# A bf16 split of K and Q moved from GpSimd to TensorE and ScalarE, and small weight operations moved from VectorE to GpSimd

## The reference

```python
def attn(Q, K, V):                     # per item and head
    scores = einsum('bhqd,bhkd->bhqk', q, k) / sqrt(16)
    return einsum('bhqk,bhkd->bhqd', softmax(scores), v)

def fp4_quant_dequant(x):              # blocks of 16 along the last dim
    scale = maximum(max(abs(xb)) / 6, 1e-12)
    q = _GRID[searchsorted(_MID, abs(xb / scale))] * sign(xb) * scale

def ffn(x, w_gate, w_up, w_down):      # 256 -> 704 -> 256
    h = silu(fp4_linear(x, w_gate)) * fp4_linear(x, w_up)
    return fp4_linear(h, w_down)

x = x + attn(layernorm(x), ctx, ctx)
x = x + ffn(layernorm(x), w_gate, w_up, w_down)
```

## Time and profile before

| | us |
|---|---|
| median of three runs | 637.24 (634.64 to 638.73) |
| the profiled execution | 639.48 |
| its span, first to last instruction | 637.7 |
| attention, filling and draining included | to about 320 |
| feed-forward | about 320 to the end |

### The profile page before, as it was taken

How to read it: one execution, slowest core, us unless ns; L and a number is a source line. 1 busy time by engine, 2 the same in 40 slices (tenths; PEclk the granted TensorE clock), 3 DMA queues, 4 the chain that set the end, 5 groups by cost and what they waited for, 6 DMA issues and landing times.

```text
span 637.7 us, 13644 instructions
## 1 busy us (share of the span) xinstructions
PE 559.7 (88%) x3780; PEld 343.7 (54%) x3780; DVE 536.4 (84%) x1186; ACT 353.4 (55%) x656; POOL 434.6 (68%) x530
## 2 busy tenths in 40 slices
PE   1479999999999999999888999999999999999996
PEld 1235545555554554555546665665665665666664
DVE  1598999999999999986578889889889889889863
ACT  1226778777777777777635355354354354354341
POOL 7787788878788888723256766766766766766740
PEclk9999999999999999999998999999999999999997
DMA  7834443444434444310000000000000000000000
GB/s 233 187 101 134 134 131 113 125 118 133 123 109 121 118 117 125 100 52 3 1 0 10 9 18 16 8 16 16 8 16 16 8 16 14 10 16 8 17 17 25
DMA packets 43797, 40.61 MB, mean 64 GB/s; under 512 B 4728, under 2 KB 43512, under 8 KB 43768
## 3 DMA queue, kind: packets, MB, share of 16 engines
q1 hardware_dynamic: 43768, 40.26, 22.3%
HBM read 10.55 MB, written 4.19 MB: 23 GB/s over the span
## 4 chain that ended last, share of the span: by engine, by line
DVE 45%; PE 25%; issue 18%; ACT 4%; DVEq 3%; POOL 2%; DMA 1%; SPq 1%; ACTq 0%; POOLq 0%
DVE MF L573 8%; DVE QS L763 7%; PE PV L906 6%; PE MX L888 5%; PE SC L874 5%; DVE hmax L773 4%; DVE hinv L641 3%; DVE KS L791 3%; PE T L810 2%; DVE hinv L645 2%; ACT QS L521 2%; PE SC L988 2%; PE T L860 2%; DVE stats L581 2%; DVE QS L719 1%
## 5 line engine op out<-in xcount | busy, mean ns | idle before, releaser
L573 DVE TENSOR_REDUCE MF<-MX 128x2 f32<-128x512 f32 x256 | 168.6, 678 | 19.6 <-PE MX L888 19.0
L482 ACT ACTIVATE P<-SC 128x512 f32<-128x512 f32 x256 | 146.6, 607 | 22.1 <-PE SC L874 20.0
L888 PE MATMUL MX<-KS,QS 96*128 96x256 bf16 x512 | 104.9, 290 | 19.3 <-DVE MF L573 15.6
L988 PE MATMUL SC<-KS,QS 128*128 128x256 f32 x384 | 93.8, 395 | 17.2 <-ACT QS L537 17.2
L874 PE MATMUL SC<-QS,KS 98*128 98x256 bf16 x512 | 100.7, 279 | 0.5 <-ACT P L482 0.5
L988 PEld LDWEIGHTS SC<-KS,QS 128*128 128x128 f32 x384 | 72.0, 194 | 42.7 <-ACT QS L537 33.8
L432 POOL TENSOR_TENSOR QS<-QS 128x256 f32<-128x256 f32 (+1 forms) x47 | 48.4, 1029 | 56.9 <-ACT QS L532 35.8
L906 PE MATMUL PV<-P,VA 128*32 128x256 f32 x1024 | 82.0, 393 | 0.7 <-ACT P L482 0.4
L888 PEld LDWEIGHTS MX<-KS,QS 96*128 96x128 bf16 x512 | 46.9, 101 | 43.7 <-DVE MF L573 34.3
L874 PEld LDWEIGHTS SC<-QS,KS 98*128 98x128 bf16 x512 | 38.3, 99 | 57.0 <-ACT P L482 36.2
L432 POOL TENSOR_TENSOR KS<-KS 128x704 f32<-128x704 f32 x16 | 26.9, 1681 | 40.9 <-ACT KS L532 40.9
(11 more groups left out here) (109 smaller groups left out, 1112.8 us busy)
## 6 DMA issues: line engine op xcount, KB each, us to landing
KS<-KP SPq DMA_DIRECT2D x96, 128.0 KB, 2.4
QS<-QP SPq DMA_DIRECT2D x96, 128.0 KB, 2.4
X<-in_x SPq DMA_DIRECT2D x16, 256.0 KB, 2.9
C<-in_ctx SPq DMA_DIRECT2D x16, 256.0 KB, 3.1
out<-KS SPq DMA_DIRECT2D x16, 128.0 KB, 1.7
out<-QS SPq DMA_DIRECT2D x16, 128.0 KB, 1.7
W<-in_L_ffn_w_down SPq DMA_DIRECT2D x1, 704.0 KB, 8.0
W<-in_L_ffn_w_gate SPq DMA_DIRECT2D x1, 640.0 KB, 5.0
```

Source lines behind the costliest of these rows:

```text
L482: nc.scalar.activation(P[g % 2][:, j, :, :], SC[h % 3][:, :, :], ACT.Exp, scale=0.25).then_inc(exp_done, 1)
L573: nc.vector.tensor_reduce(MF[st.slot(off, 2)][:, :, h:h + 1], MX[h % 2][:, :, :], AX.X, ALU.max, negate=True).then_inc(mx_done, 1)
L888: last = nc.tensor.matmul(MX[h % 2][:, q, :], QS[r][0:PROD, h, q * 128:(q + 1) * 128], KS[r][0:PROD, h, :], start=True, stop=True)
L988: last = nc.tensor.matmul(DP, HT[r][:, c, :], WDT[:, c, :], start=(c == 0), stop=(c == NT - 1))
```

## The change

K is first copied by GpSimd into head-parity order in fp32 (KN), as QN is already. `flip` transposes KN or QN in fp32 into one PSUM bank (TA for K, TB for Q). ScalarE copies the bank to bf16, which is part 0. TensorE subtracts this part from the bank by a matmul with a negative identity (`rest`), ScalarE copies again for part 1, and once more for part 2. KB, QB and REST and both splits go. The variance, the limits and the floor of the weights go from VectorE to GpSimd. Several slots move, and the maxima's transposes go from TB to TA.

```diff
@@ gpsimd, attention_step
-                    pool.wait_ge(k_tr, st.times(LEAD - 2, 2, 2))
-                    pool.wait_ge(q_parts, st.times(LEAD, 1))
+                    pool.wait_ge(k_tr, st.times(LEAD, 3))
                     gate(pool)
-                    split(lambda q: by_parity(C[rc][:, q, :]), KB[r], 0, k_parts, st)
+                    for q in range(QT):
+                        nc.gpsimd.tensor_scalar(KN[:, q, :, :, :], by_parity(C[rc][:, q, :]), 1.0, 0.0,
+                                                ALU.mult, ALU.add).then_inc(kn_ready, 1)
+                    pool.wait_ge(stats_seq, st.times(LEAD, 4, 4))
+                    gate(pool)
+                    nc.gpsimd.tensor_scalar(ve[r][:, :], mv[:, :, 1], EPS, None, ALU.add).then_inc(ve_ready, 1)
                     pool.wait_ge(ve_ready, st.times(LEAD, 1, 1))
...
-                    split(lambda q: QN[:, q, :, :, :], QB[r], 5, q_parts, st)
...
+                    pool.wait_ge(w_abs, st.times(LEAD - 1, 1, 1))
                     gate(pool)
+                    nc.gpsimd.tensor_scalar(WC[:, :], WC[:, :], MAGIC * ONE, 0.0, ALU.max, ALU.add).then_inc(w_c, 1)
...
+                    pool.wait_ge(w_seq, st.times(LEAD, 4, 1))
+                    gate(pool)
+                    for dst, up in ((wscale[st.slot(LEAD, 2)], 1), (winv, UP)):
+                        nc.gpsimd.tensor_scalar(dst[:, :], wmax[:, :], up / 6, TINY * up,
+                                                ALU.mult, ALU.max).then_inc(w_seq, 1)
                     pool.wait_ge(w_seq, st.times(LEAD, 4, 4))
@@ scalar, attention_step
-                        if (g, j) == (0, 1) and st.has(LEAD - 1):
+                        if (g, j) == (0, 0) and st.has(LEAD - 1):
...
-                        if (g, j) == (1, 0) and st.has(LEAD):
-                            part_out(KP[st.slot(LEAD, 2)], 0, k_tr, k_out, st)
-                        if (g, j) == (1, 2) and st.has(LEAD):
-                            part_out(KP[st.slot(LEAD, 2)], 1, k_tr, k_out, st)
-                        if (g, j) == (1, 0) and st.has(LEAD):
-                            part_out(KP[st.slot(LEAD, 2)], 2, k_tr, k_out, st)
-                        if (g, j) == (0, 2) and st.has(-1):
+                        for n, at in enumerate(((0, 1), (1, 0), (1, 2))):
+                            if (g, j) == at and st.has(LEAD):
+                                part_out(KP[st.slot(LEAD, 2)], TA, n, k_tr, k_out, st)
+                        if (g, j) == (0, 3) and st.has(-1):
                             evacuate(st, -1, 1)
+                        for n, at in enumerate(((2, 0), (2, 2), (3, 1))):
+                            if (g, j) == at and st.has(LEAD):
+                                part_out(QP[st.slot(LEAD, 2)], TB, n, q_tr, q_out, st)
                         if (g, j) == (2, 3) and st.has(0):
                             evacuate(st, 0, 0)
-                        if (g, j) == (3, 1) and st.has(LEAD):
-                            part_out(QP[st.slot(LEAD, 2)], 0, q_tr, q_out, st)
-                        if (g, j) == (3, 3) and st.has(LEAD):
-                            part_out(QP[st.slot(LEAD, 2)], 1, q_tr, q_out, st)
-                        if (g, j) == (3, 3) and st.has(LEAD):
-                            part_out(QP[st.slot(LEAD, 2)], 2, q_tr, q_out, st)
@@ vector, attention_step
-                        if (g, j) == (0, 2) and st.has(LEAD):
-                            variance(st)
...
-                        if (g, j) == (1, 2) and st.has(LEAD):
-                            weight_limits(st)
...
-                        if (g, j) == (2, 0) and st.has(-1):
+                        if (g, j) == (2, 1) and st.has(-1):
                             denominators(st, 0)
-                        if (g, j) == (2, 1) and st.has(-1):
                             output(st, 0)
-                        if (g, j) == (2, 2) and st.has(1):
+                        if (g, j) == (2, 3) and st.has(1):
                             maxima_out(st)
-                        if (g, j) == (2, 2) and st.has(-1):
+                        if (g, j) == (3, 1) and st.has(-1):
                             denominators(st, 1)
-                        if (g, j) == (2, 2) and st.has(-1):
                             output(st, 1)
-                        if (g, j) == (1, 3) and st.has(LEAD - 1):
-                            round_weights(st)
@@ tensor
+            def flip(bank, src):
                 for e in range(2):
                     for q in range(QT):
+                        at = e * S + q * 128
+                        last = nc.tensor.matmul(bank[:, at:at + 128], src[:, q, e, :, :].rearrange("p d a -> p (d a)"),
+                                                ident[:, :], start=(at == 0), stop=False, is_transpose=True,
+                                                skip_group_check=True)
                 return last
+            def rest(bank, part, last):
+                return nc.tensor.matmul(bank, negidentb[:, :], part, start=False, stop=last, skip_group_check=True)
+            def keys(st, n):
+                if n == 0:
+                    pe.wait_ge(kn_ready, st.times(LEAD, QT, QT))
+                    pe.wait_ge(o_norm, st.times(-1, 2))
+                    flip(TA, KN).then_inc(k_tr, 1)
+                else:
+                    pe.wait_ge(k_out, st.times(LEAD, 3, n))
+                    rest(TA, KP[st.slot(LEAD, 2)][:, n - 1, :], n == 2).then_inc(k_tr, 1)
...
             def maxima(st):
                 pe.wait_ge(m_parts, st.times(1, 1, 1))
...
+                if st.has(-1):
+                    pe.wait_ge(o_norm, st.times(-1, 2, 1))
...
             def outputs(st, q):
...
                 pe.wait_ge(o_norm, st.times(-1, 2, q))
+                if q == 1 and st.has(1):
+                    pe.wait_ge(mt_ready, st.times(1, 1, 1))
...
-                        if (g, j) == (1, 1) and st.has(LEAD):
-                            keys(st, 0)
-                        if (g, j) == (1, 1) and st.has(LEAD):
-                            keys(st, 1)
+                        for n, at in enumerate(((0, 0), (0, 3), (1, 2))):
+                            if (g, j) == at and st.has(LEAD):
+                                keys(st, n)
+                        for n, at in enumerate(((1, 3), (2, 2), (3, 0))):
+                            if (g, j) == at and st.has(LEAD):
+                                queries(st, n)
...
-                        if (g, j) == (2, 3) and st.has(-1):
+                        if (g, j) == (3, 0) and st.has(-1):
                             outputs(st, 1)
-                        if (g, j) == (3, 0) and st.has(LEAD):
-                            queries(st, 0)
-                        if (g, j) == (3, 2) and st.has(LEAD):
-                            queries(st, 1)
```

More of the change, by code:

```diff
@@ L119, in program @@
         QN = sb("QN", [128, QT, 2, DK, H // 2])
-        REST = sb("REST", [128, QT, 2, DK, H // 2])
-        KB = [sb(f"KB{r}", [128, 3, QT, 2, DK, H // 2], bf16) for r in range(2)]
-        QB = [sb(f"QB{r}", [128, 3, QT, 2, DK, H // 2], bf16) for r in range(2)]
+        KN = sb("KN", [128, QT, 2, DK, H // 2])
         KP = [sb(f"KP{r}", [128, 3, 512], bf16) for r in range(2)]
@@ L178, in program @@
         TA, TB = T[:, 0, :], T[:, 1, :]
[L179 removed]
+        TA16 = TA.bitcast(bf16)
         GP = [MX[0][:, :, :].rearrange("p q s -> p (q s)")[:, 0:FH], SC[0][:, :, :].rearrange("p q s -> p (q s)")[:, 0:FH]]
@@ L358, in _ @@
             pool.wait_ge(consts, CONSTS)
-            def split(source, parts, seq, done, st):
-                for q in range(QT):
-                    nc.gpsimd.tensor_scalar(parts[:, 0, q, :, :, :], source(q), 1.0, 0.0,
-                                            ALU.mult, ALU.add).then_inc(parts_seq, 1)
-                pool.wait_ge(parts_seq, st.times(LEAD, 10, seq + 2))
-                for q in range(QT):
-                    nc.gpsimd.tensor_tensor(REST[:, q, :, :, :], source(q), parts[:, 0, q, :, :, :],
-                                            ALU.subtract).then_inc(parts_seq, 1)
-                rest = REST[:, :, :, :, :].rearrange("p q e d a -> p (q e d a)")
-                second, third = (parts[:, n, :, :, :, :].rearrange("p q e d a -> p (q e d a)") for n in (1, 2))
-                pool.wait_ge(parts_seq, st.times(LEAD, 10, seq + 4))
-                gate(pool)
-                nc.gpsimd.tensor_scalar(second, rest, 1.0, 0.0, ALU.mult, ALU.add).then_inc(parts_seq, 1)
-                pool.wait_ge(parts_seq, st.times(LEAD, 10, seq + 5))
-                nc.gpsimd.tensor_tensor(third, rest, second, ALU.subtract).then_inc(done, 1)
             def attention_step(st):
@@ L587, in aggregate @@
                     nc.vector.bn_aggr(mv[:, q, :], stats[:, q, :]).then_inc(stats_seq, 1)
-            def variance(st):
-                dve.wait_ge(stats_seq, st.times(LEAD, 4, 4))
```

(8 more changed lines are left out.)

72 lines of the change are left out of this document (20 added, 52 removed).

## The result

The changed kernel takes 640.95 us (median of 6 runs, 638.46 to 643.13) against 635.10 for the kernel before on the same chip (6 runs, 634.02 to 638.73): ratio 1.0083, 95% interval 1.0055 to 1.011. The forecast was 633.1, that is 4.1 less than the 637.24 from which it started; it is a small loss of 5.85 us.

A forecast was written before the change was run, and what follows sets the result against it. No engine was full; order inside the step bound the kernel, then the loop through K's copy. Steps 1 to 12 -2.3, step 0 -0.5, filling -1.7, steps 13 and 14 +0.4: -4.1, 637.24 to 633.1; range 623 to 641 us.

The forecast's parts named there:

- The new wait: TensorE, before the fp32 transposes of K: waits about 1.0 us in each step for GpSimd's K copy.
- the stall before max 5: TensorE idle 0.78 us before slot 5's pair of maxima matmuls, because the variance held up reduce 3; forecast to vanish.
- The low part: VectorE's low part of the maxima: forecast to fall from 1.10 to 0.19 us once GpSimd's last split goes.
- The new loop: Repeated step, through K's copy behind the addition to X: period 13.14 + 3.88 = 17.02 us, against 17.13.
- from the start of max 13 to the transposes: From slot 13's maxima matmuls through reduction, output 1, addition and K copy to TensorE's transposes of K: 3.88 us.
- The floor: Grid floor of the weights on GpSimd: 0.45 us taken, between 0.29 and 0.79, hidden in GpSimd's idle time.
- The filling: Before step 0: -1.7 us, of which 0.1 from earlier issue, ends -0.3 and -3.
- step 0: First attention step, no additions behind it; TensorE's slower matmuls hide VectorE's gain in its first half: -0.5 us.
- A: Rival: the loop without the two waits inside it, VectorE's starts being earlier; period 16.21, 623.3 us; chance 0.22.
- B: Rival: TensorE binds, the K copy being in time; period 16.05, 622.4 us; chance 0.08.
- C: Rival: GpSimd's late weight chain holds VectorE's cast or low part, +0.8 in each of 12 steps; 641 to 643; chance 0.13.
- D: Rival: transposes and subtractions at their high ends, +0.8 us per step on TensorE; about 641; chance 0.07.

The follow-up runs named there:

- Experiment 1: Changed kernel with GpSimd's copy of K for the next item issued before both additions to X, GpSimd's program loop covering steps 1 to 8: 628.79 us, ratio 0.9855.
- Experiment 3: Changed kernel with one more half copy of K, into a buffer nobody reads, right before GpSimd's copy of K: 654.17 us, ratio 1.027.
- Experiment 8: Changed kernel with denominators and output of half 1 one slot earlier on VectorE, from (3,1) to (3,0): 631.69 us, ratio 0.9914.
- Experiment 6: Kernel before with only variance, limits and floor moved to GpSimd, the split of K and Q left there too: 672.84 us, ratio 1.0585.
- experiment 2: Changed kernel with only the grid floor of the weights back on VectorE at its old slot: 637.88 us, ratio 1.0029.
- experiment 7: Changed kernel with variance, limits and floor all back on VectorE, so only the split remains changed: 642.23 us, ratio 1.0078.

## Why the prediction was wrong

**The mechanism held.** The new wait is where the prediction put it, of the size it gave (0.92 to 1.00 against "about 1.0"), released by K's copy right behind the addition. The maxima's transposes wait for the output; the variance's 0.8 and the stall before max 5 are gone. Experiments 1, 3 and 8 show the loop causally: open it and the period falls by 1.19; lengthen it by a copy of 0.6 and it grows by 0.56 to 0.60 where TensorE's clock holds; take the output out of it and it falls by 1.02.

**Many terms were right.** K's copy with fp32 output 1.22 (1.23 taken); a subtraction of 512 columns 0.22 in the queue; a group of fp32 transposes 0.44 where nothing holds it (0.43); variance 0.23 and limits 0.31 and 0.28 (0.2 each).

**The low part.** It fell from 1.10 to 0.19, as forecast. So its length was not its own. Experiment 6 keeps GpSimd's splits but shifts them against VectorE, and there it is short as well, while the cast before it is longer (durations in ns, min/median/max, of experiment 6, and one of its steps):

```profile
L618 DVE CAST MP<-MF x16: 173/418/1090, 46.2 to 326.8; 128x32 bf16<-128x32 f32 x16
L623 DVE TENSOR_TENSOR MP<-MF,MP x16: 191/192/364, 46.6 to 327.0; 128x32 bf16<-128x32 f32 x16
...
122.12 0.62 POOL L374 TENSOR_SCALAR QB<-REST 128x512 bf16<-128x512 f32 x1 [0.20 <-POOL REST L368]
122.35 0.42 DVE L618 CAST MP<-MF 128x32 bf16<-128x32 f32 x1
122.80 0.19 DVE L623 TENSOR_TENSOR MP<-MF,MP 128x32 bf16<-128x32 f32 x1
122.82 1.19 POOL L376 TENSOR_TENSOR QB<-REST,QB 128x512 bf16<-128x512 f32 x1
```

The overlap alone doesn't hold it; what differs is which starts first. In before the low part starts 0.10 behind GpSimd's last subtraction (126.13 and 126.03) and ends 0.05 after it; here it starts 0.02 ahead of the same subtraction and takes 0.19. The Trainium skill (SBUF — State Buffer, Who interferes with whom) says that a VectorE instruction with two SBUF inputs contends with a GpSimd instruction that reads SBUF; the low part, with its two inputs, agrees. The cast has one input, and by these rows it seems held as well: it starts behind GpSimd's copy and ends 0.03 after it (122.77 and 122.74).

**What failed is the length of the loop, in sum 17.02 where 17.57 was measured.** I said I would be wrong over 17.5. The 0.55 is no single error, but more than half of it is one kind of term, the hops from one instruction to the next, and one of them I had read from the wrong place:

```
term of "The new loop"                           forecast  measured
output 1 to the addition to X                        0.09     0.19
addition and the hop to K's copy                     0.69     0.80
from the start of max 13 to the transposes           3.88     4.07
transposes of K, first slot behind the wait          0.43     0.49
normalisation's slot (beside the floor)              0.84     0.95
cast and low part                                    0.30     0.35
output to the maxima's transposes                    0.06     0.15
from the transposes to max 13                       13.14    13.51
```

The two totals hold further pieces of 0.05 and less. Three of the six single pieces, 0.30 together, are hops from a finished instruction to the next one, on another engine or on the same queue. I had priced two of them at 0.09 and 0.06 and the one from the addition to K's copy at nothing, and each came out some 0.1 longer (the last of them in nine of twelve steps; in steps 1, 5 and 9 it is 0.06).

The 0.09 stands on a row of step 13, and step 13 isn't in the program's loop. Steps 1 to 12 are three turns of a hardware loop of four steps, in which the semaphore counts to wait for and the addresses in X and W are computed from the turn; the steps behind it are written out with constants. In after, the addition that waits for VectorE's output starts 0.18 to 0.19 behind it in all twelve steps of the loop, and 0.08 to 0.09 behind it from step 13 on, as in before:

```profile
284.02 0.42 DVE L607 TENSOR_TENSOR onrm<-T,rden 128x256 f32<-128x256 f32 x1
284.52 0.72 POOL L409 TENSOR_TENSOR X<-X,onrm 128x256 f32<-128x256 f32 x1 [1.63 <-DVE onrm L607]
```

Experiment 1, whose GpSimd loop ends with step 8, shows that it is the loop and not the work in those steps. The multiplication of the weights waits for a reciprocal on VectorE. In after it starts 0.26 to 0.28 behind it in steps 1 to 12; in experiment 1 it does so in steps 1 to 8, and 0.18 to 0.19 behind it in steps 9 to 12. Step 9, first after, then experiment 1:

```profile
218.38 0.25 DVE L619 RECIPROCAL winv<-winv 128x18 f32<-128x18 f32 x1
218.91 0.68 POOL L403 TENSOR_TENSOR W<-W,winv 128x288 f32 x1 [2.75 <-DVE winv L619]
...
208.16 0.25 DVE L626 RECIPROCAL winv<-winv 128x18 f32<-128x18 f32 x1
208.60 0.68 POOL L408 TENSOR_TENSOR W<-W,winv 128x288 f32<-128x288 f32 x1 [2.76 <-DVE winv L626]
```

Which of the two computations takes the 0.1 was not tried, nor whether the other two hops have the same cause: K's copy waits for fewer semaphores than before, the maxima's transposes for one more.

A long row of short intervals, each read to 0.01, carried an error that went mostly one way, and the forecast gain of 0.11 a step was a fifth of it. The step said "nearly all that VectorE gives is taken again by one wait", and that was so; whether a little more or a little less is taken was beyond such a sum, and the sign should have been left open.

**The floor was mis-sized**, 0.45 taken with 0.79 as the high end, 1.39 measured (1.19 in the last floor, where VectorE's normalisation isn't beside it). The high end came from an operation of two inputs, as if more inputs were always dearer; the operation itself, a maximum, mattered more. It cost little here (experiment 2: 0.15 a step, from 17.57 to 17.42), less than its 1.39, because GpSimd waits 2.99 us for VectorE right behind that chain. What it cost came mostly by the normalisation beside it, which the sum had at 0.84.

**The filling** was forecast at -1.7 and came out at +0.9. Two terms are in it. The first max, forecast 0.1 earlier, came 0.9 later; it stands between 26.24 and 28.76 over the kernels here whose filling is that of the change or nearly so, released by the Q stack's transfer each time, so single executions scatter by more than the term, and what causes the scatter was not tried. The other term, -1.6 from the first max to the first scores of step 0, failed plainly: that stretch is 21.26 us in before, 21.24 in after, and 21.06 to 21.57 in the other kernels with this filling. I had credited VectorE's saved time in full, though for step 0 I had said that TensorE's slower matmuls hide it. In after's chain there, a pair of max matmuls (0.61 to 0.62) and a reduction release each other in turn, which leaves VectorE pauses that the saved time only lengthens, and the first scores wait for the transfer of the maxima, for which they had no wait in before:

```profile
48.60 0.61 PE L828 MATMUL SC<-QS,KS 98*128 98x256 bf16 x2 [0.66 <-DMA QS<-MT]
```

**The sum by its parts**: filling +0.9 for -1.7; step 0 -1.2 for -0.5; steps 1 to 12 +4.5 for -2.3; steps 13 and 14 +0.45 for +0.4. So of the 8.8 us between the forecast and these two profiles, 6.8 are the loop's and 2.6 the filling's; step 0 gave 0.7 back.

**The rivals.** A needed real starts earlier; the two waits inside the step are there (0.20 and 0.30), so it fell (its 12.33 is 12.31 by its own terms). B said that the copy would be in time; it gave 16.05 for a loop without that wait (its terms add up to 16.0), and the kernel in which the copy is in time (experiment 1) has 16.38. C said that GpSimd's weight chain would end too late: it did end at 9.8 on its scale instead of 8.6, mostly because of the floor, and the limits did lie beside the cast and the low part, but cast and low part took only 0.17 and 0.22. What stood beside them was short, and no hold of 0.8 came. Right on the time (641) by luck, C was wrong on the way, as experiments 2 and 7 show. So was D, with the same time: its high ends did not occur, a subtraction holds TensorE's queue for 0.22 and not 0.43.

## What to carry to other kernels

Before work is moved or a consumer is placed earlier in one engine's order, follow the queue of the engine that feeds it: here everything turned on one copy that needed nothing new but stood behind an addition that waited for another engine, and one reordering was worth 2.3%. A part of a change that costs nothing on one arrangement costs 6% on another (the three small moves), so measure halves of a change on both sides. When the forecast gain of a loop is far below the sum of the hops in it, price each hop from a row with the same kind of wait in the same part of the program, inside its loop or outside, and call the sign open. Credit time saved on one engine only where that engine sets the pace; in the filling it didn't.

## What was not expected of the hardware

- A maximum on GpSimd is slow: 0.93 us for 288 fp32 columns alone, 1.19 with an addition of zero behind it, against 0.62 for multiply and add on 512. In the repeated steps, beside VectorE's normalisation, both took 0.2 more, and the normalisation 0.1 more.
- The same hop from VectorE to GpSimd is 0.1 us longer in the steps of the hardware loop than in the steps written out: 0.18 to 0.19 against 0.08 to 0.09 for the addition to X, 0.26 to 0.28 against 0.18 to 0.19 for the multiplication of the weights.
- Where TensorE's wait was lengthened from 1.0 to 1.6 us, its granted clock was down to 0.60 to 0.64 over some 4 us behind four of the eleven waits, which cost more (1.3 us in such a step) than the 0.6 of the wait itself. In after, with waits of 1.0, the clock over the span was 0.995. That the wait brought the clock down is argued from the order of these rows, not shown by a run of its own, and why behind four waits only stays open: the four were 1.50 to 1.58 us long, and so were the seven others.
